# The low tail products of two neighbouring chunks in the two halves of TensorE's rows

## What is computed

```python
x = x + _L0_conv_ref(_gn(x), ...)          # spiking linear attention, 1x1 convolutions
t = _to_tokens(x)                          # [8, 1024, 192]
t = t + _L1_attn_ref(_ln_t(t), ...)        # causal softmax attention, 6 heads
t = t + _L1_ffn_ref(_ln_t(t), ...)         # four experts, two of them weighed per token
```

```python
h = gelu(einsum('bsd,edh->ebsh', x, w1) + b1)     # 192 -> 768 for each of 4 experts
y = einsum('ebsh,ehd->ebsd', h, w2) + b2          # 768 -> 192
out = einsum('bse,ebsd->bsd', masked, y)
```

## Time and profile before

| | |
|---|---|
| median of three runs | 1659.4 us |
| the profiled execution | 1659.74 us |
| its span, first to last instruction | 1657.7 us |
| TensorE busy | 1586.3 us (96%), 13274 products |
| its weight loads (beside the products) | 1034.4 us |
| VectorE busy | 1188.0 us (72%) |
| ScalarE busy | 904.0 us (55%) |
| GpSimd busy | 173.5 us (10%) |
| mean granted TensorE clock | 0.996 of full speed |

### The profile page before, as it was taken

The page is one execution under the profiler, slowest core; times in us unless marked ns, Lnnn a source line. Parts: engine busy times, 40 slices in busy tenths (PEclk is TensorE's granted clock), DMA queues, the critical chain, the costliest instruction groups (busy, mean ns, idle before and its releaser), DMA issues.

```text
span 1657.7 us, 32908 instructions
## 1 busy us (share of the span) xinstructions
PE 1586.3 (96%) x13274; PEld 1034.4 (62%) x13274; DVE 1188.0 (72%) x2537; ACT 904.0 (55%) x1329; POOL 173.5 (10%) x247
## 2 busy tenths in 40 slices
PE   3989999999999999999999999999999999999999
PEld 1534676657665576656766567665776557765676
DVE  6687786767776776867768678676777777686644
ACT  3217654466545665466554665446654566545665
POOL 2200102001210003000020010200121000300000
PEclk9999999999999999999999999999999999999999
DMA  4202002100111002010020100200011100200000
GB/s 162 59 25 65 1 1 68 35 16 2 41 28 49 1 1 68 1 49 1 1 68 1 50 2 1 67 26 25 1 38 32 49 1 1 68 1 11 1 11 10
DMA packets 25131, 47.30 MB, mean 29 GB/s; under 512 B 7410, under 2 KB 16946, under 8 KB 23700
## 3 DMA queue, kind: packets, MB, share of 16 engines
q1 hardware_dynamic: 15728, 27.85, 6.1%
q0 software_dynamic: 6144, 9.45, 2.4%
q10 hardware_dynamic: 3108, 7.91, 1.3%
HBM read 19.82 MB, written 6.29 MB: 16 GB/s over the span
## 4 chain that ended last, share of the span: by engine, by line
PE 73%; DVE 17%; ACT 5%; issue 2%; POOL 1%; DMA 1%; SPq 0%; DVEq 0%; ACTq 0%; POOLq 0%
PE ps L440 22%; PE ps L732 18%; PE ps L677 10%; PE ps L475 6%; DVE mx L1174 4%; PE ps L618 4%; PE ps L524 3%; DVE room L1361 3%; PE ps L447 2%; ACT room L900 2%; DVE norm_stats L1015 2%; ACT room L908 2%; DVE acc L1345 1%; PE ps L511 1%; PE ps L479 1%
## 5 line engine op out<-in xcount | busy, mean ns | idle before, releaser
L900 ACT ACTIVATE room<-ps,b_sb 128x512 f32<-128x512 f32 x384 | 263.1, 685 | 438.5 <-PE ps L440 438.4
L732 PE MATMUL ps<-wout_h,room 128*128 128x192 f16 x3072 | 457.2, 246 | 0.0
L1361 DVE SCALAR_TENSOR_TENSOR room<-room 128x512 f16<-128x512 f32 x384 | 263.2, 689 | 183.0 <-ACT room L908 180.8
L732 PE MATMUL ps<-wout_l,room 128*128 128x192 f16 x1536 | 377.4, 246 | 0.0
L732 PEld LDWEIGHTS ps<-wout_h,room 128*128 128x128 f16 x3072 | 285.9, 98 | 34.0 <-issue 3.2
L880 ACT ACTIVATE room<-ps 128x1024 f32<-128x1024 f32 (+3 forms) x288 | 224.8, 811 | 141.4 <-PE ps L479 104.0
L1174 DVE TENSOR_REDUCE mx<-ps 128x2 f32<-128x1024 f32 (+3 forms) x288 | 265.8, 953 | 33.7 <-PE ps L622 21.1
L908 ACT ACTIVATE room<-room 128x512 f16<-128x512 f32 x384 | 241.9, 630 | 33.6 <-PE ps L732 0.4
L677 PE MATMUL ps<-room,v 128*64 128x512 f32 (+3 forms) x1152 | 231.7, 486 | 0.9 <-DVE o L1306 0.9
L618 PE MATMUL ps<-qk 96*128 96x512 f16 (+3 forms) x576 | 151.0, 329 | 17.4 <-DVE mx L1174 10.6
L732 PEld LDWEIGHTS ps<-wout_l,room 128*128 128x128 f16 x1536 | 150.1, 98 | 27.1
(11 more groups left out here) (203 smaller groups left out, 2317.4 us busy)
## 6 DMA issues: line engine op xcount, KB each, us to landing
xc<-x_ch SPq DMA_DIRECT2D x8, 768.0 KB, 5.8
qk<-qk_all SPq DMA_DIRECT2D x96, 64.0 KB, 2.3
qk<-qk_all POOLq DMA_DIRECT2D x96, 64.0 KB, 2.5
out<-acc ACTq DMA_DIRECT2D x16, 384.0 KB, 2.6
xt<-x_tok SPq DMA_DIRECT2D x7, 768.0 KB, 7.1
qk<-qk_all POOLq DMA_DIRECT2D x96, 32.0 KB, 2.0
qk<-qk_all SPq DMA_DIRECT2D x96, 32.0 KB, 2.3
room<-w_in SPq DMA_DIRECT2D x2, 1024.0 KB, 8.5
```

Source lines behind the costliest of these rows:

```text
L732: mm = pe.matmul(dst, hid[:, s, tok], w[:, n, :], start=(k == 0 and m == 0 and t % 2 == 0), stop=False, skip_group_check=True)
L900: act.activation(h32[:, i % N_H, :], ps[:, H_BANK[i], :], ACT.Gelu, scale=1 / (U_SCALE * W_SCALE), bias=b1_sb[:, n:n + 1])\
L1361: V.scalar_tensor_tensor(out=h_l[:, s, :], in0=h32[:, s, :], scalar=A_SCALE, in1=h_h[:, s, :], op0=ALU.mult, op1=ALU.subtract)\
```

## The change

From chunk 4 of each image on, the chunks are treated in pairs of an even and the following odd one. Of an even chunk the four products other than `win_t` by `ul` are made as before. Then TensorE waits for the gelu of the chunk before (`h_act` at i), which frees the odd chunk's bank. Then two products of 64 rows are issued one after the other: rows 64 to 127 of `win_t` and `ul` for the next, odd chunk into its bank (it opens the sum there), and rows 0 to 63 for the even chunk into its own bank. `h_ps` is sent after them. An odd chunk then has four products only. The product of low weights by low tokens is left out in these chunks.

For this, the high weights of an odd chunk's tail must stand in rows 64 to 127: VectorE writes the low half in rows 64 to 127 for even chunks and for the columns ahead of the first layer, and in rows 0 to 63 for odd chunks. The weights are loaded in pieces cut at column 1860 (`COL_W1` + 10 x 128) instead of 2048, so that each holds whole pairs of chunks. Chunks 0 to 3 keep five full products, and their sums don't depend on which half of the rows holds which weights.

```diff
+PAIRED_FROM = 4
@@ build
-        pieces = [(kind, c0, min(W, IN_COLS - c0)) for kind in ("head", "tail")
-                  for c0 in range(0, IN_COLS, W)]
+        CUT = COL_W1 + 10 * P
+        pieces = [(kind, c0, w) for kind in ("head", "tail") for c0, w in ((0, CUT), (CUT, IN_COLS - CUT))]
@@ hidden(i), on TensorE
-                    project(ps[:, H_BANK[i], :], uh, ul, slice(col, col + P), slice(b * QB, (b + 1) * QB), False)\
-                        .then_inc(h_ps, 1)
+                    cols, tok = slice(col, col + P), slice(b * QB, (b + 1) * QB)
+                    if i < PAIRED_FROM:
+                        project(ps[:, H_BANK[i], :], uh, ul, cols, tok, False).then_inc(h_ps, 1)
+                        return
+                    own = ps[:, H_BANK[i], :]
+                    for m, (w, a, c) in enumerate(((win_h, uh, 0), (win_l, uh, 0), (win_h, ul, 0), (win_t, uh, 1))):
+                        mm = pe.matmul(own, w[:, cols], a[:, c, tok], start=(m == 0 and n % 2 == 0),
+                                       stop=(m == 3 and n % 2 == 1), skip_group_check=True)
+                    if n % 2 == 0:
+
+                        pe.wait_ge(h_act, at(h_act, img, i))
+                        next_cols = slice(col + P, col + 2 * P)
+                        pe.matmul(ps[:, H_BANK[i + 1], :], win_t[TAIL:P, next_cols], ul[TAIL:P, 1, tok],
+                                  start=True, stop=False, skip_group_check=True)
+                        mm = pe.matmul(own, win_t[0:TAIL, cols], ul[0:TAIL, 1, tok],
+                                       start=False, stop=True, skip_group_check=True)
+                    mm.then_inc(h_ps, 1)
@@ the low halves of the weights, on VectorE
+                if kind == "tail":
+
+                    skip = max(COL_W1 - c0, 0)
+                    if skip:
+                        V.scalar_tensor_tensor(out=win_t[TAIL:P, 0:skip], in0=stage[TAIL:P, n % 2, 0:skip],
+                                               scalar=W_SCALE, in1=win_t[TAIL:P, 0:skip],
+                                               op0=ALU.mult, op1=ALU.subtract)
+                    for odd, rows in ((0, slice(TAIL, P)), (1, slice(0, TAIL))):
+                        src = stage[rows, n % 2, skip:w].rearrange("p (k o n) -> p k o n", o=2, n=P)[:, :, odd, :]
+                        both = win_t[rows, c0 + skip:c0 + w].rearrange("p (k o n) -> p k o n", o=2, n=P)[:, :, odd, :]
+                        ins = V.scalar_tensor_tensor(out=both, in0=src, scalar=W_SCALE, in1=both,
+                                                     op0=ALU.mult, op1=ALU.subtract)
+                    ins.then_inc(stage_lo, 1)
```

More of the change, by code:

```diff
@@ L1417, in _ @@
                 dve.wait_ge(stage_hi, n + 1)
[L1418 to L1422, removed]
+                if kind == "tail":
[10 more added lines that the diff above has]
+                    ins.then_inc(stage_lo, 1)
+                else:
+                    hi = {"head": win_h, "out": wout_h_flat}[kind][:, c0:c0 + w]
+                    lo = {"head": win_l, "out": wout_l_flat}[kind][:, c0:c0 + w]
+                    V.scalar_tensor_tensor(out=lo, in0=stage[:, n % 2, 0:w], scalar=W_SCALE, in1=hi,
+                                           op0=ALU.mult, op1=ALU.subtract).then_inc(stage_lo, 1)
                 first.until(PIECE_AT[n])
```

## The result

The changed kernel takes 1662.36 us (median of 18 runs, 1661.51 to 1663.4), the one before 1659.55 us (18 runs, 1659.05 to 1661.1). The ratio is 1.0015, 95% interval 1.0008 to 1.0022: slower by 2.8 us, which is clear of zero and inside the 0.2% that was called the same. The profiled execution took 1661.74 us, with a span of 1659.7 us against 1657.7.

What follows compares the result with a forecast made beforehand. PE was taken as the bound, busy 1586 of 1657.7 us. From 1659.7: -0.5 for setup, +2.0 for seven images, +0.1 for the last gave 1661.3 us; own range 1656 to 1667, with rivals 1631 to 1675.

Steps and rivals of the forecast that it cites:

- the 0.2% that was called the same: Whole kernel: 1656.1 to 1662.7 us, 3.3 us either way, counts as the same; chance 0.46.
- A pair is one pass: Two 64-row products in an even chunk run together in 0.216 us; bound 0.43 if one after the other.
- Two changes of division at 0.22 us: In each even chunk PE goes from whole array to halves and back, costing 0.22 us; bounds 0 and 0.26.
- The rivals with the halves or the loads in a row: At each pair, second weight load queues: 1674.4 us, chance 0.12; halves run in turn, with the change: 1690.2 us, 0.08.
- those without a change: No division cost: pairs as one, 1631.8 us (0.25 together with a half-as-dear change); halves in turn, 1659.2 us, 0.05.
- What a pass is worth: One product saved per odd chunk on the chain, 0.216 us: 3.24 us an image, 22.7 in seven, 4.75 in the last.
- Where the chain leaves PE: In each of the first seven images the chain leaves PE four times; PE idles 2.5 us an image there.
- The new wait: Before an even chunk's pair PE waits for the previous chunk's gelu; 0.91 us to spare at chunk 4, cost 0.
- Off the chain, nothing: Six even chunks cost 1.32 us, seven odd save 1.51; both taken as nothing, covered by PE's idle time.
- the unbalanced even chunk of the sum: On the chain 16 even chunks cost 3.52 us an image against 3.24 saved by 15 odd: +0.28.
- Setup: At the start, new weight pieces and split tail operations change the time by -0.5 us; bounds -0.8 and +0.2.
- The last image: Its chain stays on PE; 22 changed pairs at 0.22 us cost against 0.216 saved give +0.1 us.

Runs made afterwards that it cites:

- e2: Changed kernel with only the even chunk's own half product left of each pair; 1661.7 us against 1659.91 for the kernel before.
- e3: Changed kernel with both products of each pair on rows 0 to 63; 1694.89 us against 1659.91 for the kernel before.
- e1: Changed kernel with one whole 128-row product in place of each pair, the array never divided there; 1634.74 us against 1659.91 for the kernel before.
- e6: Changed kernel with chunks 4 and 5, 42 and 43, 44 and 45 of each image unpaired; 1659.72 us against 1660.05 for the kernel before.
- e5: Kernel before with only the weight pieces cut at 1860 instead of 2048 columns; 1659.4 us against 1660.05.
- e7: Kernel before with the new weight pieces and, in the last image only, half products of four chunks per array division; 1657.64 us against 1660.05.

## Why the prediction was right, and where its terms were off

Forecast 1661.3 us, measured 1662.36. Its mechanism held: nearly all that the pair saves goes to two changes of the array's division. That the number came so close is partly luck, as said below. Point by point:

- **A pair is one pass**: right, 3 ns apart; e2 and e3 show it from both sides.
- **Two changes of division at 0.22 us**: 0.21 measured. The price taken from the columns was good to 0.01 us. The rivals with the halves or the loads in a row, and those without a change, are each excluded by the timeline. The prediction called the columns' the only change of division in the trace; there is one more, from column halves to products of 12 columns, and it reads the same, 0.15 us from start to start instead of 0.06:

```profile
519.00 0.22 PE L479 MATMUL ps<-mask_kq,identb 128*64 128x128 bf16 x2
519.16 0.39 PE L455 MATMUL ps<-ident,m 128*12 128x128 f16 x4
```

- **What a pass is worth**: the sum had 27.45 us, e1 gave 25 with the start, and 2.76 us an image instead of 3.24. PE's idle time grows in e1 from 4.2 to 5.9 us an image, so part of the saving turns into waiting.
- **Where the chain leaves PE**: a fifth place was passed over, where it runs through ACT from 483.89 to 485.79 and PE idles 1.4 us. The changed kernel is 0.57 us ahead on either side of it, so nothing of the sum hangs on it.
- **The new wait**: right. From the last whole product to the pair it is never more than 0.313 us from start to start, and in e1, with the same wait and no change of division, never more than 0.217. So ACT never held a pair up.
- **Off the chain, nothing**: this step failed in part. It took chunks 4 and 44 as covered, because PE has 0.78 and 0.82 us of idle time in these stretches. But that idle time doesn't lie behind the pair and ahead of what DVE needs from PE. In the first stretch 0.37 us of it come before chunk 4 and 0.41 at the end, in the last all 0.82 at the end, and DVE needs something from PE in between: after chunk 44 the scores that DVE reduces, after chunk 4 the attention's output for the image's other block. There DVE had almost no wait, so part of PE's 0.21 us went through, 0.10 us of it at chunk 4 and 0.13 at chunk 44. Chunk 42 was rightly on the chain without its odd partner, the unbalanced even chunk of the sum (0.2). e6 takes these three out and 0.44 us an image are gone. The sum had +0.28 an image; measured +0.47, which is 1.3 us more in seven. The distance is even larger than it looks: with the measured 0.21 and 0.2155 us the same sum gives only +0.13 an image, so that the price of 0.22 hid 1.0 us of what was missing. Of the 0.34 us an image that remain, chunks 4 and 44 are 0.23; the other 0.1 isn't placed.
- **Setup**: -0.5 forecast, -1.1 in one profile, -0.65 with an interval over zero in e5. Not settled. Of the 2.8 us between the medians, -0.4 are left for it when the images (+3.3) and the last image (-0.1) are taken as measured.
- **The last image**: +0.1 forecast. By the sum with 0.21 it is 22 x (0.21 - 0.216) = -0.1, and the traces agree: from the last front's statistics to the end it takes 300.3 us before (1357.39 to 1657.7) and 300.7 after (1359.01 to 1659.7), +0.4. As the seventh image's 0.47 is in it, -0.1 is left for the last.

So the miss of 1.3 us in the seven images is larger than the 1.1 between forecast and measurement. 0.2 in the last image and 0.15 in the start of the sum (1659.7, where the median is 1659.55) go the other way by chance, and the start of the kernel may add 0.1.

## What to carry to other kernels

Before two short products are packed into one pass of the array, look in the trace for a place where its division already changes, and price the way in and the way out there: here 0.21 us in all, as much as a pass of 512 columns. In this kernel packing paid only where one visit held more than one pair (e7), and that needs banks for more open sums. Idle time on an engine covers added work only if it lies between that work and the next result that another engine waits for; take it place by place, not as a sum over a stretch.

## What was not expected of the hardware

The way into row halves (0.096 us over the normal distance) and out of them (0.104) cost the same as for column halves in the earlier trace rows, though the loads there were of 64 columns and here of 128. And the two loads of a pair, 128 columns each for 64 rows, start together (233.20 and 233.21) and take 0.09 us as one. A second pair in the same visit, as in e7, costs 0.226 us, nearly a plain pass: the price is paid by the visit, not by the product.
